# Moving the staging transfers of the split output weights from SyncE's DMA queue to GpSimd's own

## What is computed

```python
zxbcdt = xn @ in_proj_w.T                  # gate, x, B, C, dt
xBC = silu(conv1d(xBC, conv_w) + conv_b)   # causal, 4 taps
y = chunked state-space scan(x, B, C, dt, A) + D * x
y = y * silu(gate)
y = y * rsqrt(mean over a group(y * y) + eps) * norm_w
out = hidden + y @ out_proj_w.T + ffn(xn)
```

## Time and profile before

| | us |
|---|---|
| median of 3 runs | 1989.05 (1984.93 to 1992.81) |
| the profiled execution's own time | 1983.69 |
| its span | 1982.0 |
| PE busy | 1896.8 (96%) |
| DVE busy | 1446.2 (73%) |
| ACT busy | 1164.6 (59%) |
| POOL busy | 953.6 (48%) |

### The profile page before, as it was taken

How to read it: one execution, slowest core, us unless ns; L and a number is a source line. 1 busy time by engine, 2 the same in 40 slices (tenths; PEclk the granted TensorE clock), 3 DMA queues, 4 the chain that set the end, 5 groups by cost and what they waited for, 6 DMA issues and landing times.

```text
span 1982.0 us, 28851 instructions
## 1 busy us (share of the span) xinstructions
PE 1896.8 (96%) x10416; PEld 1482.4 (75%) x10416; DVE 1446.2 (73%) x1698; ACT 1164.6 (59%) x1903; POOL 953.6 (48%) x692
## 2 busy tenths in 40 slices
PE   6998999999999999999997999999999999999986
PEld 4776767777777777777775777878787878777865
DVE  4876646867687777867674878787778787777766
ACT  2434346666777676767674666656566656565642
POOL 6566643545555454555453443444444444444432
PEclk9999999999999999999998999999999999999999
DMA  2324463455453636363645335242525252424240
GB/s 86 112 79 145 135 213 91 121 171 159 149 181 131 215 127 208 134 208 118 211 137 179 118 103 173 80 153 81 158 81 158 81 158 77 152 71 156 73 128 30
DMA packets 123100, 264.59 MB, mean 133 GB/s; under 512 B 18112, under 2 KB 24384, under 8 KB 122704
## 3 DMA queue, kind: packets, MB, share of 16 engines
q1 hardware_dynamic: 88784, 162.60, 25.9%
q10 hardware_dynamic: 34176, 100.16, 16.0%
HBM read 216.82 MB, written 45.88 MB: 133 GB/s over the span
## 4 chain that ended last, share of the span: by engine, by line
PE 71%; POOL 8%; issue 7%; DMA 7%; ACT 3%; DVE 3%; SPq 1%; ACTq 0%; POOLq 0%; DVEq 0%
PE bank L992 31%; PE bank L1047 4%; PE bank L1094 4%; PE bank L1099 4%; PE bank L1088 4%; PE bank L1012 4%; DMA wxs<-wp 4%; PE bank L1025 3%; PE bank L670 3%; PE bank L643 3%; POOL wxp L1330 3%; PE bank L1054 3%; PE bank L1037 2%; DMA wlo_scratch<-stage 2%; POOL stage L1365 1%
## 5 line engine op out<-in xcount | busy, mean ns | idle before, releaser
L992 PE MATMUL bank<-xnp,wxp 128*128 128x512 f32 x3432 | 870.8, 405 | 31.9 <-POOL wxp L1330 18.3
L992 PEld LDWEIGHTS bank<-xnp,wxp 128*128 128x128 f32 x3432 | 636.1, 189 | 192.7 <-POOL wxp L1330 35.0
L1330 POOL TENSOR_TENSOR wxp<-wxs,wxp 128x512 fp32r<-128x512 f32 x286 | 387.1, 1355 | 604.3 <-ACT wxp L1194 604.3
L1419 DVE SCALAR_TENSOR_TENSOR conv<-bank,cws,conv 128x509 f32<-128x509 f32 (+2 forms) x480 | 358.0, 746 | 11.3
L1201 ACT ACTIVATE conv<-bank,cbs,cws 128x512 f32<-128x512 f32 x160 | 124.1, 776 | 289.5 <-PE bank L992 271.1
L1360 POOL TENSOR_TENSOR yl<-gT,yh 128x1024 fp32r<-128x1024 f32 x64 | 155.3, 2427 | 210.4 <-ACT yh L1258 210.4
L1194 ACT ACTIVATE wxp<-wxs 128x512 fp32r<-128x512 f32 x286 | 178.4, 624 | 81.7 <-DMA wxs<-wp 81.5
L1506 DVE SCALAR_TENSOR_TENSOR M<-M,gb 128x1024 f32<-128x1024 f32 x128 | 184.4, 1441 | 7.5 <-DVE gb L1498 0.5
L1245 ACT ACTIVATE ya<-xT,dch 128x128 f32<-128x128 f32 x512 | 156.2, 391 | 0.0
L1094 PE MATMUL bank<-wosh,yh 128*128 128x512 f32 x512 | 136.6, 409 | 4.8 <-ACT yh L1258 4.8
L1047 PE MATMUL bank<-M,xdt 128*64 128x128 f32 x2048 | 128.2, 279 | 12.7 <-DVE acc L1527 12.7
(11 more groups left out here) (161 smaller groups left out, 2824.1 us busy)
## 6 DMA issues: line engine op xcount, KB each, us to landing
wxs<-wp SPq DMA_DIRECT2D x288, 256.0 KB, 3.6
wosh<-whi_scratch ACTq DMA_DIRECT2D x64, 512.0 KB, 6.5
wosl<-wlo_scratch ACTq DMA_DIRECT2D x64, 512.0 KB, 11.0
ecs<-ecs_scratch ACTq DMA_DIRECT2D x112, 256.0 KB, 4.8
stage<-wout SPq DMA_DIRECT2D x64, 256.0 KB, 3.2
whi_scratch<-stagh SPq DMA_DIRECT2D x64, 256.0 KB, 2.0
wlo_scratch<-stage SPq DMA_DIRECT2D x64, 256.0 KB, 2.5
wxs<-w SPq DMA_DIRECT2D x56, 256.0 KB, 2.8
```

What stands on the lines that cost most here:

```text
L992: last = pe.matmul(bank(k), wxp[:, k % 2, a, kk, :], xnp[:, b, kk, :], start=kk == 0 and a + b == 0, stop=kk == KT - 1 and a == 1)
L1330: pool.tensor_tensor(wxp[:, k % 2, 1], wxs[:, k % AHEAD], wxp[:, k % 2, 0], ALU.subtract).then_inc(w_lo, 1)
L1419: last = dve.scalar_tensor_tensor(out=conv[:, n % CB, back:], in0=bank(k)[:, 0:TH - back], scalar=cws[:, g, j, i:i + 1], in1=conv[:, n % C ...
```

## The change

fetch and keep leave SP's program for POOL's. On POOL, keep stands right behind rest_of of the same slice; fetch(two[1]) stands between the third and the fourth low; fetch of the next cell's two[0] stands behind join, ahead of combine and the fifth low. Two new semaphores, d_slice and d_kept, count the slices that POOL fetched and stored; the prologue's first eight slices stay on SP with d_raw and d_st. In the second half nothing is changed. The six transfers of a cell and their sizes are the same.

```diff
@@ sync @@
-            def fetch(n):
-
-                sp.wait_ge(d_st, 32 * n)
-                sp.dma_start(stage[:], wout[n // XT][:, n % XT]).then_inc(d_raw, 16)
-
-            def keep(n):
-
-                sp.wait_ge(st_lo, n + 1)
-                sp.dma_start(whi_dram[n // XT][:, n % XT], stagh[:].bitcast(F32)).then_inc(d_st, 16)
-                sp.dma_start(wlo_dram[n // XT][:, n % XT], stage[:]).then_inc(d_st, 16)
...
-                two = slices(q)
-                if two:
-                    fetch(two[0])
-                for i, k in enumerate(tiles_of(q)):
+                for k in tiles_of(q):
                     load_tile(k + AHEAD)
-                    if two and i == 1:
-                        keep(two[0])
-                        fetch(two[1])
-                    if two and i == 3:
-                        keep(two[1])
@@ scalar @@
             def load_high(u):
                 act.wait_ge(o_mm, done(u * CH))
-                act.wait_ge(d_st, 32 * XT * min(u + 1, G))
+                if u == 0:
+                    act.wait_ge(d_st, 32 * XT)
+                elif u < G:
+                    act.wait_ge(d_kept, 32 * XT * u)
...
-                act.wait_ge(d_raw, 16 * (n + 1))
+                act.wait_ge(d_slice, 16 * (n - XT + 1))
@@ gpsimd @@
+            def fetch(n):
+
+                if n > XT:
+                    pool.wait_ge(d_kept, 32 * (n - XT))
+                pool.dma_start(stage[:], wout[n // XT][:, n % XT]).then_inc(d_slice, 16)
+
+            def keep(n):
+
+                pool.wait_ge(st_lo, n + 1)
+                pool.dma_start(whi_dram[n // XT][:, n % XT], stagh[:].bitcast(F32)).then_inc(d_kept, 16)
+                pool.dma_start(wlo_dram[n // XT][:, n % XT], stage[:]).then_inc(d_kept, 16)
...
             join(0)
+            pool.wait_ge(d_st, 32 * XT)
+            fetch(slices(0)[0])
             for q in range(CELLS):
                 two = slices(q)
                 for k in tiles_of(q)[:2]:
                     low(k + 2)
                 if two:
                     rest_of(two[0])
+                    keep(two[0])
                 low_y(q)
-                for k in tiles_of(q)[2:4]:
+                for k in tiles_of(q)[2:3]:
+                    low(k + 2)
+                if two:
+                    fetch(two[1])
+                for k in tiles_of(q)[3:4]:
                     low(k + 2)
                 rnorm(q)
                 if two:
                     rest_of(two[1])
+                    keep(two[1])
                 if q + 1 < CELLS:
                     join(q + 1)
+                if q + 1 < CELLS and slices(q + 1):
+                    fetch(slices(q + 1)[0])
                 u, half, g, c = place(q)
                 if c == 0 and half == 0:
                     combine(g)
                 for k in tiles_of(q)[4:]:
                     low(k + 2)
```

More of the change, by code:

```diff
@@ L796, in scan @@
         built = sem("built")
+        d_slice, d_kept = sem("d_slice"), sem("d_kept")
         tap_d, conv_step, conv_d, silu_d, z_d = (
```

## The result

The changed kernel takes 2037.17 us (median of 4 runs, 2028.61 to 2041.25), the one before 1989.92 on the same chip. The ratio is 1.0235, with an interval of 1.0195 to 1.0274: slower by 47 us, as the forecast said (58 us, range 1996 to 2085).

A forecast was written before the change was run, and what follows sets the result against it. PE's list was taken as the kernel's clock. New stalls of 81.5 us, less 21.25 and 2 us won on SP, gave +58 us: median 2047 us, range 1996 to 2085.

The forecast's parts named there:

- the chain: From POOL's third low: fetch, landing, ACT's refine, rest_of, two stores, join, next fetch, last low; 13.21 us in cell 5.
- the sum of +58 us: Whole kernel: 81.5 us of new stalls, less 21.25 and 2 us won back on SP.
- d = 1.0 us: Price on POOL of each of six added DMA instructions per cell; ends 0.33 and 1.29 us.
- c = 0 to 3: Cell positions in a four-cell unit; predicted PE stalls per cell 2.94, 4.55, 1.63 and 2.94 us.
- two signs that I gave: POOL's DMA issues in the profile: about 1 us each if right, 0.4 us or less if wrong.
- covered by join: POOL's next-cell fetch waits for the stores' landing: 2.5 us from issue, hidden behind one issue and join's 2.40 us.
- The 21.25 us as won: First half, cells 1 to 27: time lost with SP's queue waiting on slices, all counted as regained.
- It may start some us earlier ... I take 2: End of first half: SP's load of xn, issued behind a store, starts 0 to about 3 us earlier.
- A: Rival, faster: POOL issues in 0.33 us and its computing does not stand for it; -10.5 us, 1978; chance 0.10.
- B: Rival, much slower: POOL's issues stretch to 2.3 us beside DVE's work; +192 us, 2181; chance 0.06.
- C: Rival, slower but less: fetch lands before ACT wants it, only POOL's own instructions count; +24 us, 2013; chance 0.12.
- D: Rival, nothing to see: issue price near 0.4 us, stalls and gain balance; 1989 us; chance 0.07.

The follow-up runs named there:

- e1: Changed kernel with fetch(two[1]) issued on POOL right behind low_y instead of behind the third low; 2000.56 us, ratio to the kernel before 1.005.
- e2: Changed kernel with each slice store cut into two halves of 128 KB, twice the store instructions on POOL, same bytes; 2068.32 us.
- e3: Changed kernel with keep(two[1]) behind the last low, fetch(two[0]) behind its own cell's first low, fetch(two[1]) behind low_y; 2050.21 us, ratio 1.0297.
- e8: e1 with the next cell's fetch behind the last low, and in c = 1 only keep(two[1]) there too; 2019.68 us, ratio 1.0176.
- e4: Kernel before, with SP's keep(two[1]) behind the next cell's first weight tile load; nothing on GpSimd's queue; 1961.28 us, ratio 0.9855.
- e5: Kernel before, with SP's keep(two[1]) in cell 27 moved behind the load of the other half of xn; 1979.46 us, ratio 0.9963.
- e7: Half of the change against the kernel before: fetches on POOL (GpSimd's queue), stores left on SP; 2018.89 us, ratio 1.015.

## Why the prediction was right, and where its sizes were off

The direction and the chain were right. That the sum of +58 us came near the measured 47 is in part luck: two errors of its sizes, each of over 30 us, went against each other.

*Direction and mechanism.* Right: PE is late for the low part of a tile because POOL's issues and a late fetch stand ahead of it. The chain is seen link by link in cell 5, and e1 (one link shortened, 37 us back) and e2 (one link lengthened, 31 us more) show that it sets most of the loss. They do not leave it alone: the clock and the landings below have their share.

*The issue, "d = 1.0 us".* This term was mis-sized: 0.56 us. The Trainium skill ("DMA: Bandwidth & Descriptors", Latency and other measured facts) has GpSimd's first byte 0.4 us behind that of SP and ACT. The traces bear this out only in part: the slice lands 3.6 us after its issue against 3.2 from SP, but at other places of GpSimd's queue it takes 3.0 to 3.1 (e1, e3, e8); the store of stagh takes 2.4 against 2.0. For the time that POOL is held the rows decide. With d = 0.56 the same working gives stalls of 1.18, 2.79, 0 and 1.62 us from c = 0 to 3, 37.5 in all, and a sum of +14. So the issue's price was 44 us too much in the sum, and what follows was missing from it. Of the two signs that I gave, issues of about 1 us and issues of 0.4 us or less, 0.56 is nearer to the wrong one.

*What was missing from the sum.* First TensorE's clock: about 15 us, since ten tiles behind a wait of 2.1 to 3.3 us run partly at 1.2 GHz. I had priced a wait at its own length. Second 0.3 us in each keep for POOL's own result, 54 times 16.0 us in all, half of it on the chain. Third the landing: 12 times POOL stood for it at the fetch, 23.6 us. Six of these, 15.3 us, are at the end of c = 3, where the sum had the landing open, at 2.5 us from the second store. The other six, 8.3 us, I had covered by join: five are at the end of c = 2. In cell 10, one of them, SP issues its store of the state and two weight tiles at the same moment (638.45 to 639.30 us, the two stores at 639.99 and 640.57), and POOL's fetch can start only at 645.48.

*By cell.* PE's waits in the changed kernel are 2.3 to 2.6 us in c = 1 (predicted 4.55), 0.7 to 2.1 in c = 2 (1.63), 2.5 to 3.3 in c = 3 (2.94), and in c = 0 0.3 to 3.3, in two cells none (2.94). c = 0 is the term furthest off: some 6 us in all where the sum had 20.6. The steps of the diagonal from c = 0 to 3 are 25.4, 32.3, 24.7 and 31.6 us in the mean, where I had named 24.7, 34.9, 24.7 and 30.9. c = 1 was put too high by the issue's price, and by the third low: in cell 5 before it ended at 482.30, 0.08 us before the square sum, and in cell 5 after at 488.71, 0.90 before it. ACT, which had stood 5.41 us for a weight tile in that cell, stands for none there any more; I take this for the reason.

*"The 21.25 us as won."* Shown in the main by e4 for the order of SP's queue: it gives 16.2 us back from cell 1 to 27, and 8.0 us of c = 1 stay. The yardstick was a little long, too. The step from c = 3 is 25.7 us in e4 where I had taken 26.30 for undisturbed; the step that I took it from, from cell 7, has a wait of PE of 0.39 us in it. So the first half of the kernel before lost some 4 us more than 21.25.

*"It may start some us earlier ... I take 2."* Mis-sized: 7.1 us in the changed kernel and 7.8 in e5. The start is only 3.3 us earlier in e5; the rest goes with ACT's load of 2 MB, which no longer runs beside it, as seen in e5. In the traces of the two kernels with 41 to 42 us (before, e7) ACT's load starts within 2 us of that of xn, in the eight with 32 to 36 us not until xn has landed or nearly has. No run moves ACT's load alone. That the store on SP is what matters is shown twice: e5 moves it and gets the time back, and e7, with its stores on SP, keeps the 41.9 us.

*Rivals.* A fell, since POOL stands for its issues. B fell: the longest fetch issue is 0.77 us, none near 2.3; nothing here shows VectorE holding up POOL's issues. Its +134 is 133 by its own d. C fell as it was put: the fetch did not land before ACT wanted it (119.6 us of ACT's waits), and its time of 2013 is 15 us under the fastest run. D fell: 0.56 us is above its 0.4, and SP's waits for the slices are gone. The rule of the Trainium skill ("DMA: Bandwidth & Descriptors", Issuing engines are not separate DMA queues), that the time of initiating is small beside the transfer, holds in size, 0.56 against 2.6 to 3.6 us. That another queue saves only this time does not hold here: what a place in a queue saves or costs is the wait that stands ahead of it, 28.6 us in e4.

*What stays open.* PE's idle time from cell 1 to 27 is 50.4 us, 47.4 of it for the low part and 3.0 for wosl, and its busy time is 691.3 where the steps without delay have 670.4. That makes the 71.3 us. Of the 20.9 us of busy time 15.5 are the ten tiles; in the kernel before PE is busy for 4.6 us more than 670.4 as well, at full clock, and that I have not traced. Nor is it shown why ten waits were followed by the lower clock and five of the same length were not. Whether some order on GpSimd's queue would beat e4 wasn't tried beyond e8.

## What to carry to other kernels

A DMA instruction that has to wait (for a result, for a landing) belongs behind everything that is ready in its queue; find what stands behind the waiting one first, since moving one load ahead of it (e4, 29 us) was worth more than another queue. An engine that also computes is a poor place for a transfer with a landing to wait for: each issue takes half a microsecond of it, and each wait what the landing takes beside the other transfers, here up to some 6 us. And "idle" in the profile of an engine is a place only if nobody else's list depends on when the transfer is done (e3, e8).

## What the runs showed of the hardware

- A DMA issue on GpSimd's queue holds POOL for 0.54 to 0.58 us in the median (0.77 at the longest) for 256 KB over 128 partitions, and for 0.54 to 0.59 us for 128 KB (e2). On SP it is 0.33 to 0.43 us in the median.
- Behind ten of fifteen waits of PE of 2.1 to 3.3 us in the changed kernel the granted clock was half for a stretch (0.72 in the mean of the 6 us from 500.00), with 12 matmuls of 128x512 in 4.3 to 5.5 us instead of 3.07.
- A store of 256 KB lands 2.6 us after its issue in the median; the one issued at 493.43 us in e8 was waited for until 499.21, with other transfers in flight.
- A fetch of 256 KB among ACT's loads of weights (eight of 512 KB) landed after 8.3 to 9.6 us in e3, in the other cells after 2.9 to 3.5.
